# A gated linear attention kernel: its level outputs as matmuls of 32 and 64 columns, in one group, with a new order of all engines

## What is computed

```python
def step(carry, xs):                      # over 512 tokens, for 16 heads of 4 sequences
    Sk, Sv = carry
    q_t, k_t, v_t, w_t, g_t, b_t = xs
    gt = jnp.exp(g_t)                     # g = log_sigmoid(h @ Wf1 @ Wf2)
    bw = b_t[:, :, None] * w_t
    Sk = Sk * gt[:, :, None, :] + k_t[..., :, None] * bw[:, :, None, :]
    Sv = Sv * gt[..., None] + bw[..., None] * v_t[:, :, None, :]
    s = jnp.einsum('bhd,bhdm->bhm', q_t, Sk) * SCALE
    a = jax.nn.softmax(s, axis=-1)
    o_t = jnp.einsum('bhm,bhmd->bhd', a, Sv)
    return ((Sk, Sv), o_t)
```

## Time and profile before

| | us |
|---|---|
| median of three runs | 2792.84 |
| the profiled execution | 2791.86 |
| its span, first to last instruction | 2790.1 |
| TensorE busy | 2741.3 (98%) |
| VectorE busy | 2247.3 (81%) |
| ScalarE busy | 1629.7 (58%) |
| GpSimd busy | 1420.1 (51%) |

### The profile page before, as it was taken

How to read it: one execution, slowest core, us unless ns; L and a number is a source line. 1 busy time by engine, 2 the same in 40 slices (tenths; PEclk the granted TensorE clock), 3 DMA queues, 4 the chain that set the end, 5 groups by cost and what they waited for, 6 DMA issues and landing times. The chain is left out here.

```text
span 2790.1 us, 42861 instructions
## 1 busy us (share of the span) xinstructions
PE 2741.3 (98%) x13558; PEld 1910.1 (68%) x13558; DVE 2247.3 (81%) x5841; ACT 1629.7 (58%) x3649; POOL 1420.1 (51%) x2122
## 2 busy tenths in 40 slices
PE   6999899999999999999999999999999999999999
PEld 5888566666666666666666666666666666666887
DVE  7554689988888999888889998888898999884543
ACT  5111676677666666776666767666766666661110
POOL 0200366666666666665666666656666666661000
PEclk9999999999999999999999999999999999999999
DMA  4500211111112111111121111111211111105000
GB/s 170 196 16 16 79 35 36 35 50 35 49 35 65 55 61 35 50 35 50 35 73 50 58 35 50 35 50 35 80 50 58 35 51 37 50 29 193 16 16 31
DMA packets 90929, 151.03 MB, mean 54 GB/s; under 512 B 9296, under 2 KB 30928, under 8 KB 90192
## 3 DMA queue, kind: packets, MB, share of 16 engines
q1 hardware_dynamic: 90704, 148.29, 16.7%
HBM read 127.02 MB, written 21.23 MB: 53 GB/s over the span
## 5 line engine op out<-in xcount | busy, mean ns | idle before, releaser
L946 POOL TENSOR_TENSOR s<-s,tmp 128x256 f32<-128x256 f32 (+1 forms) x448 | 358.8, 801 | 312.0 <-DVE tmp L1258 276.1
L1611 PE MATMUL ps<-rows_even,standing 128*128 128x512 f32 x1024 | 498.1, 595 | 2.7 <-ACTq L1062 2.7
L1611 PE MATMUL ps<-hT,standing 128*128 128x512 f32 x1024 | 497.4, 593 | 0.0
L946 POOL TENSOR_TENSOR X<-S,D 128x256 f32<-128x256 f32 x384 | 278.8, 726 | 97.2 <-ACT S L1121 73.2
L1654 PEld LDWEIGHTS ps<-Y,S 128*128 128x128 f32 x1536 | 221.3, 191 | 153.1 <-issue 135.5
L946 POOL TENSOR_TENSOR Y<-aT,D 128x256 f32<-128x256 f32 x384 | 280.3, 751 | 0.0
L341 ACT ACTIVATE sig<-up_ps 128x512 f32<-128x512 f32 x88 | 52.6, 597 | 389.8 <-PE up_ps L570 389.8
L946 POOL TENSOR_TENSOR A<-ident,dg 128x512 f32<-128x512 f32 x64 | 66.7, 1041 | 380.3 <-DVE standing L1348 356.9
L1642 PEld LDWEIGHTS ps<-AM,XT 128*128 128x128 f32 x1536 | 211.6, 191 | 64.1 <-issue 60.2
L1258 DVE TENSOR_TENSOR tmp<-ps,D 128x256 f32<-128x256 f32 (+1 forms) x448 | 196.2, 438 | 63.7 <-PE ps L1642 47.6
L1587 PE MATMUL ps<-standing,og 128*128 128x512 f32 x480 | 245.2, 593 | 0.0
(11 more groups left out here) (215 smaller groups left out, 6679.5 us busy)
## 6 DMA issues: line engine op xcount, KB each, us to landing
standing<-in_wk_dram SPq DMA_DIRECT2D x64, 256.0 KB, 2.5
standing<-in_ww_dram SPq DMA_DIRECT2D x64, 256.0 KB, 2.6
standing<-in_wq_dram SPq DMA_DIRECT2D x64, 256.0 KB, 2.7
standing<-in_wv_dram SPq DMA_DIRECT2D x64, 256.0 KB, 2.8
standing<-in_wo_dram SPq DMA_DIRECT2D x64, 256.0 KB, 3.3
wq_dram<-wq SPq DMA_DIRECT2D x3, 2816.0 KB, 20.0
space<-in_w_dram SPq DMA_DIRECT2D x8, 704.0 KB, 11.1
x_sb<-in_x_dram SPq DMA_DIRECT2D x4, 1024.0 KB, 5.6
```

The lines of the kernel that those rows point to most:

```text
L946: return nc.gpsimd.tensor_tensor(out, in0, in1, op)
L1611: mm = nc.tensor.matmul(bank[x][:, :], ck_(slot[x], kk), hT[n // NH % 2][:, kk, :], start=(kk == 0), stop=(kk == KT - 1))
```

## The change

1. `outputs(l)`: for the levels 1 to 32 each of the two matmuls becomes four, with 32 columns of weights (32 sources, written to 32 partitions of PSUM) and the 32 targets of the same blocks. Level 64 becomes two of 64 and 64 each. What lies outside is not computed; the masks drop it as before.
2. The outputs of the levels 1, 2, 16, 32, 8, 4 follow each other in TensorE's order without anything between them; level 64 comes later. The results of all levels have their own halves of banks.
3. `S` of the levels 1, 2, 4, 8 exists twice, for even and odd units.
4. All engines have a new order. On VectorE `add_diagonal` comes ahead of the first convolution of k, the four `diagonal_outputs`, `diagonal_scores` are placed one by one, and the merges stand between other operations than before. On GpSimd the Y are made in the order 2, 8, 16, 32, 4, 64.

```diff
+TWICE = (1, 2, 4, 8)
+def source_parts(l):
+    width = P // 2 if l == 64 else P // 4
+    return [(p0, p0 + width) for p0 in range(0, P, width)]
+
+def target_part(t, l, i, j, rows=(0, P)):
+    if l == 64:
+        return rows_pat(t, *rows, j * P + i * (P // 2), (1, P // 2))
+    if l == 32:
+        return rows_pat(t, *rows, (j % 2) * P + i * (P // 2) + (j // 2) * (P // 4), (1, P // 4))
+    return rows_pat(t, *rows, i * (P // 2) + j * (P // 8), (P, 2), (1, P // 8))
+
+def odd_target_part(t, i, j):
+    return pat(t, 1 + i * P + j * (P // 4), (HALF - 1, 2), (2, P // 8))
...
-        S = {l: sb(f"S{l}", [P, HALF]) for l in LEVELS}
+        S = [{l: sb(f"S{l}", [P, HALF]) for l in LEVELS}]
+        S += [S[0] | {l: sb(f"S{l}b", [P, HALF]) for l in TWICE}]
...
+        for l, (i, half) in {1: (0, 0), 2: (0, 1), 4: (1, 0), 8: (1, 1), 16: (5, 0), 32: (5, 1), 64: (6, 0)}.items():
+            bank[f"a2_{l}"] = psum[i][:, half * HALF:(half + 1) * HALF]
...
                 def outputs(l, done):
                     for i in range(2):
-                        last = nc.tensor.matmul(pair_columns(bank[f"a2_{l}"], i), ck_(S[l], i),
-                                                odd_targets(aT, i) if l == 1 else pair_columns(Y[l], i),
-                                                start=True, stop=True)
+                        for j, (p0, p1) in enumerate(source_parts(l)):
+                            last = nc.tensor.matmul(target_part(bank[f"a2_{l}"], l, i, j, (p0, p1)),
+                                                    ck_(S[u % 2][l], i)[:, p0:p1],
+                                                    odd_target_part(aT, i, j) if l == 1 else target_part(Y[l], l, i, j),
+                                                    start=True, stop=True)
                     last.then_inc(done, 1)
...
-PE_LATE = "skT s16 s32 sst s64 sT aT a2_1 a2_2 a2_4 a2_8 a2_16 a2_32 a2_64 o onT".split()
+PE_LATE = "s16 skT s32 sst s64 sT aT a2_1 a2_2 a2_16 a2_32 a2_8 a2_4 a2_64 o onT".split()
```

More of the change, by code:

```diff
@@ L1390, in turn @@
                     norm_rows(n // NH + 1, 3)
+                if late:
+                    dve.wait_ge(pe_late, after(PE_LATE, "sT", u))
+                    add_diagonal(3)
+                    add_diagonal(0)
+                    add_diagonal(1)
+                    add_diagonal(2)
+                    dve.wait_ge(dve_late, after(DVE_LATE, "sx2", u))
+                    nc.vector.tensor_reduce(nmx[:, :], st[:, :, :], AX.X, ALU.max,
+                                        negate=True).then_inc(dve_late, 1)
+                    dve.wait_ge(dve_late, after(DVE_LATE, "mx", u))
+                    nc.vector.tensor_scalar(nms[:, :], nmx[:, :], SCALE, None, ALU.mult).then_inc(dve_late, 1)
                 if early:
@@ L1404, in turn @@
                     conv("k", 2)
+                if late:
+                    dve.wait_ge(act_late, after(ACT_LATE, "e3", u))
+                    diagonal_outputs(3)
+                    dve.wait_ge(act_late, after(ACT_LATE, "e2", u))
+                    diagonal_outputs(2)
+                    dve.wait_ge(act_late, after(ACT_LATE, "e0", u))
+                    diagonal_outputs(0)
+                if early:
                     dve.wait_ge(dve_early, after(DVE_EARLY, "ck2", n))
@@ L1435, in turn @@
                 if late:
-                    dve.wait_ge(pe_late, after(PE_LATE, "a2_8", u))
-                    dve.wait_ge(dve_late, after(DVE_LATE, "a2_4", u))
-                    merge(8)
+                    dve.wait_ge(pe_late, after(PE_LATE, "a2_2", u))
+                    merge(1)
                 if early:
+                    dve.wait_ge(dve_early, after(DVE_EARLY, "cq1", n))
+                    conv("q", 2)
+                if late:
+                    dve.wait_ge(dve_late, after(DVE_LATE, "a2_1", u))
+                    merge(2)
+                if early:
+                    dve.wait_ge(dve_early, after(DVE_EARLY, "cq2", n))
+                    conv("q", 3)
+                    dve.wait_ge(act_early, after(ACT_EARLY, "h2", n))
+                    dve.wait_ge(pool_late, after(POOL_LATE, "y4", u))
+                    decays(2)
                     if n == 0:
@@ L1524, in turn @@
                     end_state(2, dve_early)
-                    masked(16, dve_early)
+                if late:
+                    dve.wait_ge(pe_late, after(PE_LATE, "onT", u))
+                    gated_even()
+                if early:
+                    dve.wait_ge(pe_early, after(PE_EARLY, "s8", n))
                     dve.wait_ge(pool_early, after(POOL_EARLY, "ad2", n))
@@ L1628, in transpose_sources, with transpose_into_upper @@
                 def transpose_sources(l, done):
-                    transpose(f"x{l}T", lambda i: ck_(S[l], i), done, 2)
+                    transpose(f"x{l}T", lambda i: ck_(S[n % 2][l], i), done, 2)
+                def transpose_into_upper(into):
+                    for c in range(2, C):
+                        nc.tensor.transpose(ck_(into, c), ident[:, :], ident[:, :])
                 def chunk_scores(done):
@@ L1753, in turn @@
                     project("v", 0)
-                if late:
-                    pe.wait_ge(pool_late, after(POOL_LATE, "y8", u))
-                    outputs(8, pe_late)
-                if early:
-                    pe.wait_ge(act_early, after(ACT_EARLY, "w", n))
+                    pe.wait_ge(act_early, after(ACT_EARLY, "we", n))
                     transpose("wT", lambda c: ck_(w, c), pe_early)
@@ L1762, in turn @@
                     project("v", 1)
-                if late:
-                    pe.wait_ge(dve_late, after(DVE_LATE, "a2_4", u))
-                    pe.wait_ge(pool_late, after(POOL_LATE, "y16", u))
-                    outputs(16, pe_late)
-                if early:
                     project("v", 2)
+                    project("v", 3)
                 if late:
@@ L1771, in turn @@
                         pe.wait_ge(act_early, after(ACT_EARLY, "xt0", n))
-                    pe.wait_ge(pool_late, after(POOL_LATE, "y32", u))
-                    outputs(32, pe_late)
-                if early:
-                    project("v", 3)
-                if u >= C:
-                    out_rows(u - C, bank["out"], 0)
-                if late:
                     pe.wait_ge(pool_late, after(POOL_LATE, "y64", u))
@@ L1786, in turn @@
                     transpose("kT", lambda c: ck_(k, c), pe_early, C - 1)
-                    pe.wait_ge(act_early, after(ACT_EARLY, "q", n))
-                    chunk_scores(pe_early)
+                if u >= C:
+                    out_rows(u - C, bank["out"], 1)
                 if late:
```

339 lines of the change are left out of this document (161 added, 178 removed), and 6 rows, old and new, of the table bank.

## The result

The changed kernel takes 2743.99 us (median of four runs, 2742.5 to 2744.29), beside 2793.78 us of the kernel before on the same chip: a ratio of 0.9823, 95% interval 0.9806 to 0.984. The forecast was 2748, in a range of 2712 to 2845. The profiled execution has a span of 2742.3 us. That is 0.79 us a turn or 51 us in 64 turns, which covers the whole difference of 50 us.

A forecast was written before the change was run, and what follows sets the result against it. TensorE was taken as the bound; −1.14 for the parts, +0.33 for changes of the array's division and +0.10 for the Y4 wait gave −0.71 us a turn, −45 us over 64 turns, 2748 us, range 2712 to 2845.

The forecast's parts named there:

- What bounds the kernel: Whole turn: TensorE, busy 400.00 of 400.00 us in the attention phase, sets the time unless another engine becomes too late.
- the 99% that was named as a sign of a wrong sum: TensorE's busy share in the middle: below 99% with waits for VectorE, the sum would be wrong.
- The parts: Output matmuls cut into strips on TensorE: 1.98 us a turn instead of 3.12, a gain of 1.14.
- the middle case: Parts in different strips: a part's second pass follows its first, so a part costs one pass and gap, 0.036 us.
- The best case: Parts wholly beside each other, only one strip's time counts: 0.98 us a turn, a gain of 2.1.
- The changes of the division: TensorE going from whole array to strips and back twice a turn: 0 to 0.66 us, middle taken, a loss of 0.33.
- The wait for the Y: TensorE's group of levels waiting for GpSimd's Y4: 0 to 0.3 us a turn, a loss of 0.1.
- rival 4: Strips wholly beside each other, gain held by Y4 and VectorE to 1.0 to 1.2 us a turn: 2716 to 2728; chance 0.12.
- the first (serial): Rival that strips on TensorE don't overlap: +0.33 to +0.99 us a turn, 2814 to 2856; chance 0.23.
- VectorE and GpSimd apart: Reordered VectorE merges and decays avoiding GpSimd: 0 to 1.5 us a turn less on VectorE, none TensorE time, price 0.
- The floor of 33.5 us a turn: VectorE's work of 30.4 us plus waits of 3.06 us a turn: there VectorE would become the bound.
- Rival 2: Each short TensorE pass has a floor of 0.06 us: 5.8 us against 2.67, +220 us, 3010; chance 0.08.

The follow-up runs named there:

- e2: The changed kernel with the outputs as two whole matmuls a level again, the new order kept: 2794.45 us, no difference from the kernel before.
- e11: e9 with q's second tap on VectorE moved ahead of the merge of level 1: 2736.34 us.
- e3: The changed kernel with every part's results in the first PSUM partitions, so all passes of 32 use one strip of the array: 2854.38 us.
- e1: The kernel before with only the outputs cut into parts, in its old order with the levels at six places: 2789.72 us.
- e8: The changed kernel with r1 moved behind Y64 on GpSimd and level 64 as two whole matmuls again: 2730.66 us.
- e7: The changed kernel with r1 behind Y64 on GpSimd and level 4 moved out of the group to stand beside level 64: 2732.97 us.
- e10: e7 with v's second projection matmul moved ahead of the transposes of w: 2732.61 us.
- e12: e11 with VectorE's merge of level 16 shrunk to 8 columns, leaving out that level's outputs: 2745.80 us.
- e9: e8 with v's first projection matmul moved ahead of the group of six levels and the second ahead of the transposes of w: 2741.53 us.

## Why the prediction came out right

The time was hit within 4 us (2748 against 2743.99), but by terms of which two were wrong and cancelled, and a third was a middle taken without a reason.

**What bounds the kernel.** Right. All of the gain is TensorE's time in the two places, and e2 shows that the order alone is worth nothing. TensorE's share in the middle, 397.03 of 400 us, stayed over the 99% that was named as a sign of a wrong sum.

**The parts: mis-sized.** Forecast 1.98 us a turn for 104 passes (1.73 for the group, 0.25 for level 64), a gain of 1.14. Without waits the group takes 1.04 (e11) and level 64 0.38, together 1.42, a gain of 1.70. The step that failed is the reason for the middle case, "the second pass of a part uses the same strip as the first and must follow it, but the next part's first pass uses another strip and can start with it". I took from it that a part costs one streaming time. Measured, four passes share the time of one (four starts 7 ns apart, the next four 0.032 us later), so a part of two passes costs half a streaming time. The starts don't alternate between 0.03 us and a few ns as forecast, and the group takes 1.59 us with its waits, under the 1.7 to 2.1 named. Which pass belongs to which part the trace doesn't tell, so why the second pass holds up nothing is not shown. e3, with everything in one strip, costs 0.032 a pass, the price that I had for a serial pass; that bound was exact. The best case was nearest, with a remainder of about 0.3 us for the group over 0.75 (a quarter of 2.98) and of 0.15 for level 64 over 0.23.

**The changes of the division: right, by luck.** Forecast 0.33 us; by starts 0.10 + 0.10 at the group and 0.10 + 0.06 at level 64, 0.36. The forecast was the middle of 0 to 0.66, taken because no row spoke for either end; the 0.66 that it read from the rule on draining is not reached. The cost itself agrees with the Trainium skill, TensorEngine Tiling (Array Packing), Key Properties, that a change of the mode drains the array: e1 puts the whole price of a place, with what its last passes need to drain, at 0.33 us.

**The wait for the Y: mis-sized.** Forecast 0.10 for Y4, measured 0.55 for Y32 and Y4 together. The arrival of Y4 was read about rightly, but the group reaches it earlier because the parts are faster; and Y32, which stands behind r1 too, was not looked at (0.21 us from start to start). The prediction had this for its rival 4 ("wait 1 us") and held the best case to 1.0 us a turn by it.

**The sum.** −1.70 + 0.36 + 0.55 = −0.79 us a turn, against −0.71. The errors of the parts (−0.56) and of the wait (+0.45) have one cause and opposite signs: a wait behind a step takes up what the step gains beyond the forecast. That is why the total was insensitive to the wrong middle case. Of the rivals, the fourth had the mechanism and the first (serial) was e3. Rival 4's 2716 to 2728 left out that the changes of the division are paid on top: −2.1 + 0.33 + 1.0 = −0.8 us a turn, about 2743, was what its own terms gave.

**VectorE and GpSimd apart: price 0, right.** D<-u_g went to 634 ns, not to 420, and the share of VectorE stayed at 350.42 of 400 us, 88% and not 90%, which is 29.6 us of a turn of 33.80 against 30.4 before. The floor of 33.5 us a turn was stated for VectorE alone. The variants that took waits off TensorE stopped at 33.59 to 33.64 (e8, e7, e10). But what stops them isn't VectorE's sum alone: e11 and e12 show paths over ScalarE, VectorE and GpSimd that all start at the transposes of w and end within some 0.1 to 0.3 us of each other. In e8 itself TensorE still has one wait of note, 0.41 us a turn for Y4 by starts (18.6 us by the table), and e7, e9 and e10, without it, are no faster than e8; how low the turn could go is open. A kernel with v's first matmul ahead of the group and the transposes of w directly behind it wasn't tried.

**Rival 2, a floor of 0.06 us a pass: refuted.** The prediction gave it 0.08. Beside it stood two rules of the Trainium skill, TensorE: Matmul & The Clock Gate, section "Wait — 56ns, not 53.3ns?": some 62 ns of sequencer time for a MATMUL with hardware decoding off, and never less than about 25 ns from start to start. The group's 96 passes in 1.04 us, 0.011 us apart on average, are far under both, so for parts in different strips the 25 ns don't hold; whether hardware decoding was on no run tells. The prediction also said that the 25 ns would leave its sum as it is, which was a slip: its 1.73 us for 96 passes are 0.018 a start, and 96 starts 0.025 apart would take 2.4 us.

## What to carry to other kernels

When a block-diagonal product is cut into parts for column strips of the array, count the places, not only the passes: here a place costs about 0.33 us for entering, draining and leaving, a level in it 0.13 to 0.16 us against 0.445 whole, so one level alone brings nothing and six together save over one microsecond. Before taking the gain, find what the next step waits for: the group outran the GpSimd products it needs, and the waits for them gave back 0.55 us, as large as any other term. And look at what a filler delays before using it to cover a wait: v's matmul ahead of the transposes of w covered one wait and started the chains behind w late.

## What was not expected of the hardware

Passes of 32 columns in different strips can be 0.011 us apart on average over 96 of them, and 7 ns within a four, where the same passes in one strip are 0.032 apart. A fp32 matmul's two passes don't hinder this. Time that GpSimd seems to lose to VectorE does not go away when the operation that lost it is moved: 0.19 us went from r1 (386 to 200 ns) to Y32 (732 to 917 ns), with D<-u_g left where it was. And less work on VectorE made a kernel slower (e12, 9 us).
